# Row sums of a split weight matrix moved behind the split, in a mixing and low-rank-expert kernel

## The reference, cut to what matters

```
att   = softmax(mlp(cond))                       # 32 x 8
agg_w = einsum('bk,koi->boi', att, weight)       # a 64 x 64 matrix per batch
agg_b = att @ bias_k                             # a bias per batch and channel
y     = einsum('boi,bih->boh', agg_w, x) + agg_b[:, :, None]
out   = y @ W_base.T + moe_lora(y; gate_W, A, B) # softmax gate, top 2 of 8, rank 8 each, scaling 2
return x + out
```

## Time and profile before

| | |
|---|---|
| median of 3 runs | 265.97 us (265.45 to 266.51) |
| profiled execution, its span from first to last instruction | 265.7 us |
| its own time, as near as the runs tell | 265.45 to 266.51 us, up to 0.8 us around the span |
| TensorE busy | 254.0 us, 96% |
| VectorE, ACT, GpSimd busy | 53%, 26%, 25% |

### The profile page before, as it was taken

The page is one execution under the profiler, slowest core; times in us unless marked ns, Lnnn a source line. Parts: engine busy times, 40 slices in busy tenths (PEclk is TensorE's granted clock), DMA queues, the critical chain, the costliest instruction groups (busy, mean ns, idle before and its releaser), DMA issues.

```text
span 265.7 us, 4272 instructions
## 1 busy us (share of the span) xinstructions
PE 254.0 (96%) x1451; PEld 247.9 (93%) x1451; DVE 141.1 (53%) x398; ACT 69.0 (26%) x156; POOL 65.2 (25%) x46
## 2 busy tenths in 40 slices
PE   8699679999999999999999999999999999999994
PEld 5498678999999999999999999999999999999993
DVE  2998999446536345434445363454344453634542
ACT  4539034131313122131213131221312231311110
POOL 3657688030210303040302103040304021030000
PEclk9999795999999999999999999999999999999999
DMA  6998020042423060606042240606060332404012
GB/s 199 400 379 286 0 79 1 0 160 96 144 97 140 15 222 1 237 0 216 21 150 86 79 158 9 228 0 237 0 205 32 129 108 74 163 18 142 0 79 79
DMA packets 9527, 31.02 MB, mean 117 GB/s; under 512 B 1072, under 2 KB 1584, under 8 KB 9520
## 3 DMA queue, kind: packets, MB, share of 16 engines
q1 hardware_dynamic: 9520, 30.93, 33.3%
HBM read 22.54 MB, written 8.39 MB: 116 GB/s over the span
## 4 chain that ended last, share of the span: by engine, by line
PE 85%; DVE 9%; DMA 2%; ACT 2%; SPq 1%; issue 1%; DVEq 0%; ACTq 0%
PE z_ps L660 23%; PE z_ps L662 23%; PE z_ps L661 23%; PE o_ps L679 3%; DVE w_lo L455 3%; PE o_ps L690 3%; PE o_ps L688 3%; PE o_ps L676 3%; PE o_ps L674 3%; DMA w_raw<-wext_in 2%; DVE b_lo L607 1%; ACT w_hi L335 1%; DVE blk_lo L467 1%; DVE gate L509 1%; DVE lora_split L517 1%; DVE att_rep L569 1%
## 5 line engine op out<-in xcount | busy, mean ns | idle before, releaser
L660 PE MATMUL z_ps<-w_hi,xt_hi 128*128 128x366 f32 (+1 forms) x384 | 130.8, 341 | 4.1 <-DVE w_lo L455 4.0
L662 PE MATMUL z_ps<-w_hi,xt_lo 128*128 128x366 f32 (+1 forms) x384 | 129.1, 336 | 0.0
L661 PE MATMUL z_ps<-w_lo,xt_hi 128*128 128x366 f32 (+1 forms) x384 | 128.9, 336 | 0.0
L660 PEld LDWEIGHTS z_ps<-w_hi,xt_hi 128*128 128x128 f32 x384 | 74.4, 194 | 6.0 <-DVE w_lo L455 5.0
L460 DVE TENSOR_TENSOR z_lo<-z_ps,z_hi 128x366 fp32r<-128x366 f32 (+1 forms) x48 | 25.8, 538 | 96.4 <-ACT z_hi L341 96.3
L296 POOL TENSOR_TENSOR xt_lo<-xt_raw,xt_hi 128x1024 fp32r<-128x1024 f32 x14 | 36.8, 2628 | 154.3 <-ACT xt_hi L331 154.3
L661 PEld LDWEIGHTS z_ps<-w_lo,xt_hi 128*128 128x128 f32 x384 | 74.6, 194 | 0.0
L662 PEld LDWEIGHTS z_ps<-w_hi,xt_lo 128*128 128x128 f32 x384 | 74.2, 193 | 0.0
L341 ACT ACTIVATE z_hi<-z_ps 128x366 fp32r<-128x366 f32 (+1 forms) x48 | 22.8, 475 | 149.9 <-PE z_ps L662 149.8
L476 DVE SCALAR_TENSOR_TENSOR x_nat<-w_sum,bias,x_nat 128x1024 f32<-128x1024 f32 (+2 forms) x18 | 23.0, 1280 | 3.8 <-DMA x_nat<-x_in 3.8
L531 DVE TENSOR_TENSOR out_sb<-o_ps,x_nat 128x366 f32<-128x366 f32 (+1 forms) x44 | 19.9, 505 | 4.7 <-PE o_ps L690 3.8
(11 more groups left out here) (94 smaller groups left out, 170.0 us busy)
## 6 DMA issues: line engine op xcount, KB each, us to landing
x_nat<-x_in SPq DMA_DIRECT2D x16, 512.0 KB, 4.6
xt_raw<-xt_in SPq DMA_DIRECT2D x15, 512.0 KB, 5.1
out<-out_sb SPq DMA_DIRECT2D x15, 512.0 KB, 3.0
w_raw<-wext_in SPq DMA_DIRECT2D x8, 366.0 KB, 8.7
w_raw<-wext_in SPq DMA_DIRECT2D x4, 364.0 KB, 5.8
par<-small_in SPq DMA_DIRECT2D x1, 576.0 KB, 7.4
xt_raw<-xt_in SPq DMA_DIRECT2D x2, 256.0 KB, 4.2
out_sb<-bt_in SPq DMA_DIRECT2D x2, 256.0 KB, 12.3
```

Source lines behind the costliest of these rows:

```text
L660: nc.tensor.matmul(dst, hi, w_cols(w_hi, g, k), start=(k == 0), stop=False)
L661: nc.tensor.matmul(dst, hi, w_cols(w_lo, g, k), start=False, stop=False)
L662: last = nc.tensor.matmul(dst, lo, w_cols(w_hi, g, k), start=False, stop=(k == KC - 1))
```

## The change

The folds on GpSimd wait until VectorE has made all of w_lo, and their groups are interleaved with x_low of tiles 2 and 3. The 72 gate and expert sums no longer come by way of the folds: one VectorE reduction (g_part) adds the eight chunks of the raw columns, and one fp32 matmul with ones sums over the partitions; ACT copies the result to the first 72 columns of w_sum. The other sums move one to two tiles later: row_sums(0) into z(1,2), row_sums(1) behind tile 1's transpose, row_sums(2) into tile 2's step; their `part_high` and `sum_copy` on ACT move likewise. Because w_sum's 1024 columns are then not there in time for tiles 0 and 1, x_bias of these two tiles is replaced by `late_bias`, which adds bias times w_sum in out_sb after the sum o + x_nat has been written there, in VectorE's step of tile 2; the stores of tiles 0 and 1 wait for it. The two-tile step pair 1 leaves the loops of ACT, TensorE and GpSimd and is written out.

```diff
@@ SP
-            def step(j, parity, load_t=True, load=True):
+            def step(j, parity, load_t=True, load=True, keep=False):
...
                 sp.wait_ge(evacuated, G * t)
-                sp.dma_start(out_t[t - 1], out_sb[:, 1 - parity, :]).then_inc(out_stored[1 - parity], 16)
+                if not keep:
+                    sp.dma_start(out_t[t - 1], out_sb[:, 1 - parity, :]).then_inc(out_stored[1 - parity], 16)
...
-            step(0, 1, load_t=False)
-            step(1, 0, load_t=False)
+            step(0, 1, load_t=False, keep=True)
+            step(1, 0, load_t=False, keep=True)
+            for t in range(2):
+                sp.wait_ge(late_biased, t + 1)
+                sp.dma_start(out_t[t], out_sb[:, t, :]).then_inc(out_stored[t], 16)
             step(1, 1)
@@ GpSimd
+            nc.gpsimd.memset(ones_32[:, :], 1.0).then_inc(ones32_ready, 1)
...
-            for g in range(G):
-                fold_group(g)
-            with pool.Fori(1, PAIRS) as j:
+            pool.wait_ge(w_lo_ready, PIECES)
+            fold_group(0)
+            x_low(2, 0)
+            fold_group(1)
+            x_low(3, 1)
+            fold_group(2)
+            with pool.Fori(2, PAIRS) as j:
@@ ACT
-            def step(j, parity, last=False):
+            def step(j, parity, last=False, sums=False):
...
                 nc.scalar.activation(lora_t[:, :], t_ps[:, 0:P], ACT.Copy).then_inc(lora_t_ready, 1)
+                if sums:
+                    sum_copy(1)
                 if not last:
                     x_high(j + parity, 1 - parity)
                 z_high(t, 0)
                 block_high(t, parity)
+                if sums:
+                    part_high(2)
...
-                if g == 2:
-                    part_high(0)
...
-            sum_copy(0)
+            act.wait_ge(g_sum_mm, 1)
+            nc.scalar.activation(w_sum[:, 0:GZ], s_ps[:, GS:GS + GZ], ACT.Copy).then_inc(g_sum_ready, 1)
             x_high(0, 1, first=True)
...
             ratio_exp(0)
-            part_high(1)
...
-            sum_copy(1)
             x_high(1, 0)
             block_high(1, 1, first=True)
             z_high(1, 0)
-            part_high(2)
+            part_high(0)
             z_high(1, 1)
+            sum_copy(0)
             ratio_exp(1)
+            part_high(1)
+            step(1, 0, sums=True)
             sum_copy(2)
-            with act.Fori(1, PAIRS - 1) as j:
+            step(1, 1)
+            with act.Fori(2, PAIRS - 1) as j:
@@ VectorE
+            def late_bias(t):
+                nc.vector.scalar_tensor_tensor(out_sb[:, t, :], w_sum[:, GZ:NCOL], bias[:, t:t + 1], out_sb[:, t, :],
+                                               ALU.mult, ALU.add).then_inc(late_biased, 1)
...
                 z_low(t - 1, 2)
-                x_bias(j, parity)
+                if not early:
+                    x_bias(j, parity)
                 z_low(t, 0)
                 block_low(t, parity)
-                add_out(j - 1 + parity, 1 - parity, first=early)
-                if last:
+                add_out(j - 1 + parity, 1 - parity, first=early, early=early)
+                if early:
+                    z_low(t, 1)
+                    gating(t)
+                    dve.wait_ge(sum_ready, G)
+                    late_bias(0)
+                    dve.wait_ge(evacuated, 2 * G)
+                    late_bias(1)
+                    x_bias(j, parity)
+                elif last:
...
+            nc.vector.tensor_reduce(g_part[:, :],
+                                    w_raw[:, 0:KC * WIDTH[0]].rearrange("p (k c) -> p c k", k=KC)[:, 0:GZ, :],
+                                    AX.X, ALU.add).then_inc(g_part_ready, 1)
             w_low(PER_G)
...
-            dve.wait_ge(sum_ready, 1)
+            dve.wait_ge(g_sum_ready, 1)
             gating(0)
...
-                dve.wait_ge(sum_ready, g + 1)
-                x_bias(0, 0, cols)
-                dve.wait_ge(x_biased, g + 1)
                 dve.wait_ge(main_done, g + 1)
...
+            dve.wait_ge(xn_loaded[0], 16)
             first_tile_out(0)
...
             first_tile_out(2)
-            x_bias(0, 1)
@@ TensorE
             pe.wait_ge(bias_ready, 2)
-            row_sums(0)
+            pe.wait_ge(ones32_ready, 1)
+            pe.wait_ge(g_part_ready, 1)
+            nc.tensor.matmul(s_ps[:, GS:GS + GZ], ones_32[:, :], g_part[:, :], start=True, stop=True).then_inc(g_sum_mm, 1)
             pe.wait_ge(agg_ready, NG // AGG_BANK)
             o_group(0, 0, 0, bank_free=True)
...
             transpose_lora(0)
-            row_sums(1)
...
             z_group(1, 1, 2, chunks=range(KC // 2))
-            row_sums(2)
+            pe.wait_ge(bias_ready, 2)
+            pe.wait_ge(g_sum_ready, 1)
+            row_sums(0)
             z_group(1, 1, 2, chunks=range(KC // 2, KC), bank_free=True)
             o_group(1, 1, 1)
             transpose_lora(1)
-            with pe.Fori(1, PAIRS - 1) as j:
+            row_sums(1)
+            step(1, 0, sums=True)
+            step(1, 1)
+            with pe.Fori(2, PAIRS - 1) as j:
```

More of the change, by code:

```diff
@@ L45 @@
 AGG_BANK = 2
+GS = 160
 G = 3
@@ L88, in build @@
         fold = sb("fold", [P, PC * max(WIDTH)])
+        g_part = sb("g_part", [P, GZ])
         w_part = sb("w_part", [P, NCOL])
@@ L109, in build @@
         ones_r = sb("ones_r", [P, P], F32R)
+        ones_32 = sb("ones_32", [P, P])
         att_max = sb("att_max", [BATCH, 1])
@@ L151, in build @@
         ones_ready = sem("ones_ready")
+        ones32_ready = sem("ones32_ready")
         zeros_ready = sem("zeros_ready")
@@ L167, in build @@
         w_lo_ready = sem("w_lo_ready")
+        g_part_ready = sem("g_part_ready")
+        g_sum_mm = sem("g_sum_mm")
+        g_sum_ready = sem("g_sum_ready")
+        late_biased = sem("late_biased")
         fold_step = sem("fold_step")
@@ L358, in sum_copy @@
                 act.wait_ge(sum_mm, g + 1)
-                nc.scalar.activation(z_cols(w_sum, g), s_ps[:, 0:WIDTH[g]], ACT.Copy).then_inc(sum_ready, 1)
-            def step(j, parity, last=False):
+                nc.scalar.activation(w_sum[:, FIRST[g] + SKIP[g]:FIRST[g] + WIDTH[g]], s_ps[:, SKIP[g]:WIDTH[g]],
+                                     ACT.Copy).then_inc(sum_ready, 1)
+            def step(j, parity, last=False, sums=False):
                 t = 2 * j + parity
@@ L520, in gating, with add_out @@
                                         ALU.subtract).then_inc(gate_step, 1)
-            def add_out(j, parity, first=False, groups=range(G)):
+            def add_out(j, parity, first=False, groups=range(G), early=False):
                 t = 2 * j + parity
-                dve.wait_ge(x_biased, t + G)
+                if early:
+                    dve.wait_ge(xn_loaded[parity], 16)
+                else:
+                    dve.wait_ge(x_biased, t - 1)
                 if not first:
@@ L697, in transpose_lora, with row_sums, step @@
                                  start=True, stop=True).then_inc(lora_t_mm, 1)
-            def step(j, parity):
+            def row_sums(g):
+                if g > 0:
+                    pe.wait_ge(sum_ready, g)
+                pe.wait_ge(part_lo_ready, g + 1)
+                nc.tensor.matmul(s_ps[:, 0:WIDTH[g]], ones_r[:, :], z_cols(part_hi, g), start=True, stop=False)
+                nc.tensor.matmul(s_ps[:, 0:WIDTH[g]], ones_r[:, :], z_cols(part_lo, g),
+                                 start=False, stop=True).then_inc(sum_mm, 1)
+            def step(j, parity, sums=False):
                 t = 2 * j + parity
@@ L707, in step @@
                 z_group(t, parity, 2)
+                if sums:
+                    row_sums(2)
                 o_group(t, parity, 1)
                 transpose_lora(t)
[L711 to L716, removed]
-                nc.tensor.matmul(s_ps[:, 0:WIDTH[g]], ones_r[:, :], z_cols(part_lo, g),
-                                 start=False, stop=True).then_inc(sum_mm, 1)
             def warm(n):
```

## The result

| | before | changed |
|---|---|---|
| first comparison, 4 runs each | 266.24 us (265.45 to 267.88) | 263.78 us (262.45 to 264.85) |
| ratio, 95% interval | | 0.9897 (0.985 to 0.9944) |
| compared once more, beside the experiments, 6 runs against 11 | 267.05 us | 262.53 us, 0.9842 (0.9802 to 0.9883) |
| span of the profiled execution | 265.7 us | 261.6 us |

The account below looks back on a forecast made before the run. TensorE, busy 254.0 of 265.7 us, was taken to lose time waiting for w_lo that GpSimd's folds delayed. Gains of 7.3 (A to C) less 0.7, 0.4 and 1.0 (D to F) gave 260.8 us, range 256.2 to 264.8.

Parts of the forecast that it names:

- B: End of z(0,0) to o(0,1): w_lo comes in time, z(0,2) falls from 8.44 us to 4.05; gain 4.4, worst 3.0.
- C: From o(0,1) to o(0,2)'s third matmul: folds meet gating(0), TensorE idles 2.0 us, b_lo takes 1.28; gain 1.2, ends 0.2 and 3.5.
- A: Start to the end of z(0,0): w_lo without folds beside it, third chunk at 10.06; gain 1.7 us, ends 1.2 and 2.5.
- gate sum's reduction: VectorE's new reduction ahead of w_lo 4: about 0.75 us, from 0.3 to 2.8, cost 0 at both ends.
- D: From o(0,2)'s third matmul to tile 2: gating(1) collides with the second fold group; loss 0.7 us, range +1 to -3.
- E: Tile 2: row_sums(2) adds 0.35 us on TensorE, part_hi(2) makes ACT wait; loss 0.4 us, ends 0.3 and 3.
- rival 3: A third stretch at 1.2 GHz after the idle time of D or F gives back 3 us: 263.8; chance 0.20.
- F: Tile 3: stores and load_xt(4) wait for late_bias(1), delaying xt_hi(4) and o(3,0); loss 1.0 us, ends 0 and 2.5.
- The step from span to time: The forecast span of 260.5 us became a median time of 260.8 by adding 0.27 us.
- Rival 1: Clock stays up: gating(0) slips through, no 1.2 GHz stretch follows, C and D gain more; 257.0 us, chance 0.22.
- Rivals 2 and 4: 2: folds too late for ACT's fixed order, 269.2 us, chance 0.07; 4: start bound elsewhere, about 266, chance 0.03.

Follow-up runs that it names:

- e2: Changed kernel without GpSimd's wait for all of w_lo, so the first group's folds start early; 265.66 us, ratio 0.992 to the kernel before.
- e7: e6 with the first folds waiting for the end of gating(0) instead of the end of w_lo; 260.38 us, ratio 0.9758 to the kernel before.
- e6: e5 plus gating(1)'s exponential ahead of the first sum copy and row_sums(1) with its copy behind z(2,0); 258.88 us, unedited second run 258.75.
- e9: e6 with each GpSimd fold issued as two ops of half the width; 259.57 us, ratio 0.9701 to the kernel before.
- e3: Changed kernel with ACT's exponential of gating(1) ahead of the copy of the first row sums; 263.10 us, ratio 0.9815 to the kernel before.
- e8: The changed kernel, unedited, run once more beside the others; 262.53 us, ratio 0.9842 to the kernel before.
- e1: Changed kernel with tile 4's load of transposed x issued ahead of the two stores that wait for late_bias; 264.26 us, ratio 0.9853 to the kernel before.
- e5: Changed kernel with tile 4's load ahead of the late stores and z_lo(2,2) ahead of late_bias on VectorE; 260.58 us, ratio 0.9762 to the kernel before.
- e4: Changed kernel with ten matmuls that compute nothing needed ahead of tile 1's transpose; 264.94 us, ratio 0.9897 to the kernel before.

## Why the prediction was right, and where it was not

**The bound and steps B and C held, and A by luck in its size.** GpSimd's folds beside VectorE's SBUF ops were what made w_lo late: the pieces are ordinary without them, and e2 brings a piece of 2.43 us back with the first group. In A the third chunk began at 10.03, where 10.06 was worked out; but the matmul distance fell from 0.30 to 0.17 us after 13.48, where the prediction had 15.5 or 16.6, and that earlier date, not the folds, makes the difference between 2.25 and 1.7. The end of z(0,0) varies by 2.5 us between executions of the same code (last section), so against the same profile of before A could have come out anywhere from 1.1 to 3.7. Two slips in the sums are small: fifteen matmuls of 0.30 us from 11.7 end at 16.2, not 16.4, and by B's own dates C starts at T + 11.8, not T + 11.65. z(0,2) fell from 8.44 to 4.03 us (22.34 to 26.37), as worked out; B's other 0.8 us is the border between z(0,1) and z(0,2), 1.50 before and 0.72 now, which the prediction had left as it was. Of the time that z(0,2) lost before, some 1.5 us were a stretch at 1.2 GHz behind its two waits, in this window of the kernel before:

```profile
30.00:35.00 5.00, 4.86 (x20) 4.86 (x21) 4.60 (x15) 1.67 (x4) 1.68 (x2) 0.66 0.24 71
```

In C the transpose waits 1.76 us where 2.0 were forecast, b_lo takes 1.22 us instead of 2.78, and the third matmul of o(0,2) comes at 33.75, just ahead of the 34 to 36 that were to show it right. The gate sum's reduction took 1.24 us (0.75 was taken, bounds 0.3 to 2.8) and cost nothing, since VectorE still idled behind it.

The plainest case of a small op behind a whole GpSimd op is e7's: 1.71, 1.64 and 1.63 us, each beside a fold of 1.8. The Trainium skill ("SBUF — State Buffer", section "SBUF: two separate sides") says that the shared port pair is held for a whole instruction; these rows agree. What decided more was the count: gating(0) in the changed kernel and both gatings in e6 and e9 ended within 0.4 us of the closing add, gating(1) in e7 within 0.1 of the last fold, wherever the run was put and however it was cut. That is no rule: in the kernel before, gating(0) ended at 39.02, while a run of folds went on until 42.40.

**D's sum was right, its working was not.** The prediction had the transpose held by folds alone, and row_sums(1) a little longer. Tile 2 began at 47.41, where 47.5 to 50 had been named. The prediction overlooked that ACT's exponential of gating(1) was now queued behind sum_copy(0), which waits for row_sums(0) in the middle of z(1,2): 1.90 us of VectorE's time. e3 shows why the sum came out all the same: part_lo(1) was late to the same date, and takes over as soon as the other wait goes.

**E was mis-sized, 1.78 for 0.4.** The term was right as far as it went (row_sums(2) on TensorE, part_hi(2) hidden); what it lacked is a stretch of 1.2 GHz behind the 2.35 us wait, 1.5 us by the distances and 1.54 by the comparison with e8, where it did not follow. That was rival 3, with a chance of 0.20 and a price of 3 us: it came about in this execution at half the price.

**F was mis-sized, 2.37 for 1.0, inside its ends of 0 and 2.5, and is the step that failed.** The mechanism was right: load_xt(4) behind late_bias in SP's queue, ACT and the block copies behind it. The load was issued 3.0 us after tile 3's start (3.1 forecast), and xt_hi(4) began 7.4 us after it, earlier than the 8.2 forecast; yet o(3,0) began at 11.8, where 10.7 was forecast. Two things behind xt_hi(4) had been put at nothing. VectorE's block_low(3) met GpSimd's xt_lo(4), which the same load released, and took 1.93 us, where e1, with xt_lo(4) out of the way, has 0.46; and o(3,0) waits not for the block alone, but for add_out(2) too, which is queued behind it. e1 shows that a second wait, on z_lo(2,2), stands ready as soon as this one goes, and e5 what both are worth: 1.95 us.

**The step from span to time was wrong.** The prediction added 0.27 us to its span. In every execution with both numbers the time lies 1.7 to 2.4 us above the span (263.55 at 261.6 for the changed kernel's profile, 265.70 at 263.6 for one run of the kernel before). The profiled execution of before, with span 265.7, thus took an estimated 267.7 us and was one of the slow end, about 1.5 us above the median of the first comparison, so that the 4.1 us between the two profiles overstate the first comparison (2.5) and lie near the second (4.5).

Rival 1 came about by half: no stretch at 1.2 GHz followed the transpose of tile 0 (granted clock 1.00 in the windows from 20 to 45 us), though it waited 1.76 us, and in the kernel before one had followed 1.71. But gating(0) did not slip through, and D did not gain: TensorE arrived early and stood 2.35 us before tile 1's transpose instead. Rivals 2 and 4 did not come about: a fold group takes 6.5 us beside gating(1), not 9.7, and behind part_hi(1) and part_hi(2) z_hi and x_hi still came in time for TensorE.

## What to carry to other kernels

Work on GpSimd beside VectorE's SBUF ops cost here by what it lay beside, not by its length: beside long ops that TensorE awaits it stretched them two- to threefold, and moved elsewhere it found the next awaited chain. Before moving it, list for each engine's in-order queue what short, awaited instruction will stand behind the moved one (here an exponential behind a sum copy, a z_lo behind late_bias, a load behind a store): those three reorderings, with row_sums(1) moved as in e6, add no work and brought 3.65 us on top of the 4.5 that the change gave in the same comparison. And where a wait goes and the time stays, look for the second wait that ended at the same date before giving up the edit.

## What the runs showed of the hardware that was not expected

The date at which TensorE's matmuls first come at their short distance differs from execution to execution. The distance falls from 0.30 to 0.17 us after 16.64 in the kernel before, after 13.48 in the changed one, and the end of z(0,0) lies between 13.9 (the second run of e6) and 16.5 us (e9) in versions whose code is the same up to there. That alone is 2.5 us, as much as the change's gain in the first comparison. That it is the clock is read from the distance: in these two profiles the granted clock shows 1.00 in all windows up to 20 us, but in e4 and the first run of e6, where the same matmuls come 0.30 us apart, it shows 0.50 in 10 to 15 us.

Stretches at 1.2 GHz follow some waits and not others of the same length: behind 2.35 us at tile 1's transpose in the changed kernel, not behind 2.34 in e8; behind 1.76 us at tile 0's transpose in e5 (granted clock 0.69 in 30 to 35 us), not behind 1.76 in the changed kernel. What decides the one or the other is left open, and so is their part in the spread between runs: of the ten runs of the changed kernel the three with a mean granted clock of 1.000 took 262.47 to 264.01 us, the three with 0.987 took 262.39 to 264.85. In the same way runs of the kernel before with a mean of 1.000 took 266.61 to 267.75 us, those with 0.980 or 0.981, the profiled one's mean, 266.15 to 268.18. Taken together the runs do not show that what a stretch loses where it stands is still lost at the end, though e8 fits it: its span is 1.0 us shorter than the changed kernel's first, from a start 0.5 later.

The later tiles of the changed kernel take 14.61 us each, before 14.64, from transpose to transpose; that is the 0.4 us of the last row of the account, and has no cause that these traces show.
